# Two pairs per output product, and the output bias moved from TensorE to POOL

## The reference

```python
x = x + tanh(g_xattn[0]) * xattn(layernorm(x), ctx_1024, ctx_1024, Wq, Wk, Wv, Wo)   # 16 heads of 64
x = x + tanh(g_ffn[0]) * ffn(layernorm(x), ...)

def ffn(x):
    h = rmsnorm(x, gamma1)
    q = (h @ Wq + bq).reshape(b, t, 16, 8)
    kv = ((h @ Wdown + bdown) @ Wup + bup).reshape(b, t, 16, 16)
    k, v = split(kv, 2, axis=-1)
    att = softmax(einsum('bthd,btgd->bthg', q, k) / sqrt(8))
    x = x + (einsum('bthg,btgd->bthd', att, v).reshape(b, t, 128) @ Wo + bo)
    h2 = rmsnorm(x, gamma2)
    gate = softmax(h2 @ Wg + bg)                        # 8 experts
    return x + einsum('btd,edf,bte->btf', h2, We, gate)
```

## Time and profile before

| | us |
|---|---|
| three runs | 260.14, 260.2, 263.66 |
| median | 260.2 |
| the profiled execution | 261.93 |
| its span | 259.9 |

### The profile page before, as it was taken

How to read it: one execution, slowest core, us unless ns; L and a number is a source line. 1 busy time by engine, 2 the same in 40 slices (tenths; PEclk the granted TensorE clock), 3 DMA queues, 4 the chain that set the end, 5 groups by cost and what they waited for, 6 DMA issues and landing times.

```text
span 259.9 us, 7887 instructions
## 1 busy us (share of the span) xinstructions
PE 245.6 (94%) x3244; PEld 178.7 (69%) x3244; DVE 192.4 (74%) x333; ACT 171.6 (66%) x501; POOL 149.9 (58%) x157
## 2 busy tenths in 40 slices
PE   7989989998899999999999999988999897979995
PEld 4765877785867677676859595858676462858774
DVE  0237644189998989898998842799989999786964
ACT  2437634756687787978787778566877676472454
POOL 4104041264646686969696835778466995867320
PEclk9999999999999999999999999999999998899999
DMA  6990000000000000000000000000000000000000
GB/s 208 359 320 21 3 4 3 3 1 3 3 3 0 3 10 3 15 0 15 1 3 13 3 11 3 13 3 10 3 0 5 11 14 3 11 0 3 10 13 20
DMA packets 6017, 7.30 MB, mean 28 GB/s; under 512 B 477, under 2 KB 4830, under 8 KB 5982
## 3 DMA queue, kind: packets, MB, share of 16 engines
q1 hardware_dynamic: 5550, 6.16, 7.5%
q10 hardware_dynamic: 432, 0.64, 0.7%
HBM read 5.88 MB, written 0.92 MB: 26 GB/s over the span
## 4 chain that ended last, share of the span: by engine, by line
PE 70%; DVE 18%; ACT 5%; issue 4%; POOL 1%; DVEq 0%; POOLq 0%
PE ps_a L875 40%; PE ps_c L875 9%; PE ps_b L875 8%; PE ps_e L875 7%; PE ps_b L927 4%; DVE ps_e L665 3%; DVE prod L683 3%; DVE ps_e L694 2%; ACT probs L446 2%; DVE nmax L626 2%; PE ps_b L872 1%; DVE psums L631 1%; DVE fqkv L649 1%; POOL prod L326 1%; PE ps_c L971 1%
## 5 line engine op out<-in xcount | busy, mean ns | idle before, releaser
L326 POOL TENSOR_TENSOR prod<-fqkv 128x1280 f32<-128x1280 f32 (+1 forms) x14 | 38.7, 2761 | 10.3 <-DVE fqkv L649 10.3
L316 POOL TENSOR_TENSOR probs<-probs,prinv 120x672 f32<-120x672 f32 x16 | 24.3, 1518 | 31.1 <-DVE prinv L635 31.1
L334 POOL TENSOR_TENSOR prod<-e_sb,fqkv 128x768 f32<-128x768 f32 (+1 forms) x14 | 24.5, 1753 | 21.3 <-ACT e_sb L474 21.3
L875 PEld LDWEIGHTS ps_a<-aT,wo_sb 128*128 128x128 f32 x256 | 30.8, 196 | 4.4 <-ACT v_sb L435 2.6
L875 PE MATMUL ps_a<-aT,wo_sb 128*128 128x112 f32 x256 | 32.1, 279 | 0.4 <-ACT aT L440 0.3
L875 PE MATMUL ps_a<-wv_sb,cT 128*64 128x512 f32 x128 | 32.3, 620 | 0.0
L665 DVE TENSOR_REDUCE ps_e<-prod 128x256 f32<-128x2048 f32 x13 | 29.7, 2287 | 0.0
L694 DVE TENSOR_REDUCE ps_e<-prod 128x128 f32<-128x2048 f32 x13 | 29.7, 2285 | 0.0
L875 PE MATMUL ps_a<-cT,wk_sb 128*128 128x224 f32 x128 | 28.6, 375 | 0.0
L429 ACT COPY kT<-ps_a 128x448 f32<-128x448 f32 x32 | 17.1, 533 | 16.2 <-PE ps_a L875 16.2
L875 PE MATMUL ps_a<-xT,wqc 128*128 128x224 f32 x128 | 27.1, 361 | 0.6 <-ACT qT L429 0.6
(11 more groups left out here) (144 smaller groups left out, 487.9 us busy)
## 6 DMA issues: line engine op xcount, KB each, us to landing
xp_sb<-in_xp SPq DMA_DIRECT2D x1, 896.0 KB, 7.9
out<-out_sb SPq DMA_DIRECT2D x14, 64.0 KB, 1.5
xT<-in_x_t SPq DMA_DIRECT2D x1, 784.0 KB, 9.5
cT<-in_ctx_t SPq DMA_DIRECT2D x1, 784.0 KB, 11.1
wv_sb<-in_wv SPq DMA_DIRECT2D x1, 512.0 KB, 8.1
wo_sb<-in_wo SPq DMA_DIRECT2D x1, 512.0 KB, 12.7
fwe_sb<-in_fwe SPq DMA_DIRECT2D x1, 512.0 KB, 8.8
fw_sb<-in_fw SPq DMA_DIRECT2D x1, 266.0 KB, 13.1
```

The lines of the kernel that those rows point to most:

```text
L316: nc.gpsimd.tensor_tensor(pr[0:TG, NC:C, :, 0:S], pr[0:TG, NC:C, :, 0:S], prinv[p % 2][0:TG, NC:C, :].unsqueeze(3).to_broadcast([TG, C - N ...
L326: nc.gpsimd.tensor_tensor(o, k, q, ALU.mult).then_inc(s["prod1_pool"], 1)
L334: nc.gpsimd.tensor_tensor(o, e, v, ALU.mult).then_inc(s["prod2_pool"], 1)
L875: return nc.tensor.matmul(o, lhsT, rhs, start=start, stop=stop, skip_group_check=True)
```

## The change

Three things are changed. The output products of pairs 1-2, 5-6, 7-8 and 9-10 are made two pairs at a time, 224 columns wide; those of pairs 3, 4 and 11 to 16 stay single (`Y_UNITS`, which counts from 0). So the two buffers of aT become one with two halves. A tile can start only when the unit that completes it is there: the tiles now start in slots 2, 3, 4, 6, 7, 8, 9 and 10 to 16, and slot 5 has no new tile instead of slot 9; slots 5, 7 and 9 have no output product. The bias matmul goes: ACT scales xc by rstd2 (`scaled_x`), POOL adds bo to it (`biased`), and `new_x2` only adds. And the order within a slot is new on every engine.

```diff
-def first_step(f):
-    return (128 * (f + 1) + T - 1) // T
-TILE_AT = {first_step(f): f for f in range(NT)}
+Y_UNITS = [(0, 1), (2,), (3,), (4, 5), (6, 7), (8, 9)] + [(p,) for p in range(10, NP)]
+Y_AT = {unit[-1] + 1: n for n, unit in enumerate(Y_UNITS)}
+def units_for(f):
+    return next(n + 1 for n, unit in enumerate(Y_UNITS) if (unit[-1] + 1) * T >= (f + 1) * 128)
+def tile_steps():
+    steps, last = {}, 0
+    for f in range(NT):
+        last = max(last + 1, Y_UNITS[units_for(f) - 1][-1] + 1)
+        steps[last] = f
+    return steps
+TILE_AT = tile_steps()
...
-        aT = two("aT", [128, C, T])
+        aT = sb("aT", [128, C, 2 * T])
...
+            def biased(f):                                   # POOL
+                pool.wait_ge(s["u_ready"], f + 1)
+                if f == 0:
+                    pool.wait_ge(s["wo_scaled"], 2)
+                nc.gpsimd.tensor_tensor(xc[f % XB][:, :], xc[f % XB][:, :], fw_sb[:, COL_BO:COL_BO + D], ALU.add).then_inc(s["ub_ready"], 1)
...
+            def scaled_x(f):                                 # ACT
+                act.wait_ge(s["centred"], f + 1)
+                act.wait_ge(s["rstd2_ready"], f + 1)
+                nc.scalar.activation(xc[f % XB][:, :], xc[f % XB][:, :], ACT.Copy, scale=rstd2[f % XB][:, 0:1]).then_inc(s["u_ready"], 1)
...
             def new_x2(f):                                   # VectorE
                 dve.wait_ge(s["o_made"], f + 1)
-                nc.vector.scalar_tensor_tensor(out=x2[f % 2][:, 0:D], in0=xc[f % XB][:, :], scalar=rstd2[f % XB][:, 0:1], in1=ps_c[:, 1, 0:D],
-                                               op0=ALU.mult, op1=ALU.add).then_inc(s["x2_ready"], 1)
+                dve.wait_ge(s["ub_ready"], f + 1)
+                nc.vector.tensor_tensor(x2[f % 2][:, 0:D], ps_c[:, 1, 0:D], xc[f % XB][:, :], ALU.add).then_inc(s["x2_ready"], 1)
...
-            new_x1(0)                                        # VectorE, ahead of the slots
...
-            def new_y(p):                                    # TensorE
+            def new_y(n):
...
+                c0, w = Y_UNITS[n][0] % 2 * T, len(Y_UNITS[n]) * T
                 for ch in range(C):
-                    ins = mm(ps_a[:, 0, 0:T], wo_sb[:, ch, :], aT[p % 2][:, ch, :], start=(ch == 0), stop=(ch == C - 1))
+                    ins = mm(ps_a[:, 0, 0:w], wo_sb[:, ch, :], aT[:, ch, c0:c0 + w], start=(ch == 0), stop=(ch == C - 1))
...
-                mm(ps_c[:, 1, 0:D], ident[:, :], fw_sb[:, COL_BO:COL_BO + D], stop=False)
...
-            new_y(0)                                         # TensorE, between attend(0) and attend(1)
```

More of the change, by code:

```diff
@@ L408, in _ @@
             gating(third)
+            biased(prior)
             weighted(last)
+            biased(last)
             second_scale(prior)
@@ L545, in _ @@
                     squares(fc)
+                if t < NP:
+                    exps(t)
+                if fc is not None:
                     x2_copy(fc)
@@ L550, in _ @@
                     head_exps(fb)
+                if fc is not None:
+                    gate_exps(fc)
+                if fb is not None:
+                    scaled_x(fb)
                 if t < NP:
@@ L564, in _ @@
                     kv_copy(fa)
+                if fc is not None:
+                    experts(fc, 1)
             for t in range(TAIL, END):
@@ L586, in _ @@
             x1_copy(last)
+            squares(third)
             kv_copy(last)
+            head_exps(prior)
             x2_copy(third)
-            squares(third)
-            head_exps(prior)
-            late_out(PE_OUT[0])
+            scaled_x(prior)
             gate_exps(third)
@@ L798, in _ @@
                     new_x2(fc)
+                if fb is not None:
+                    logits(fb)
+                if t in Y_AT:
+                    new_x1(Y_AT[t])
                 if t < NP:
                     prob_sums(t)
-                if t <= NP:
-                    new_x1(t - 1)
-                if t < NP:
                     norm(t)
                 if fb is not None:
-                    logits(fb)
                     shifted_logits(fb)
@@ L847, in _ @@
             weighted(prior)
+            gate_logits(third)
             logits(last)
-            gate_logits(third)
+            gate_sum(third)
             shifted_logits(last)
             head_scales(prior)
-            gate_sum(third)
             normed_heads(prior)
             weighted(last)
+            head_scales(last)
             new_x2(prior)
-            head_scales(last)
             head_sums(last)
@@ L1099, in _ @@
                 if t < NP:
+                    values(t, 1)
+                if fc is not None:
+                    new_o(fc)
+                if t < NP:
                     shift(t)
-                if fc is not None:
-                    bias_o(fc)
-                    new_o(fc)
-                if t <= NP:
-                    new_y(t - 1)
+                if t in Y_AT:
+                    new_y(Y_AT[t])
                 if fc is not None:
@@ L1118, in _ @@
                     first(fa)
+                if t < NP:
+                    turn_probs(t)
                 if fc is not None:
```

119 lines of the change are left out of this document (57 added, 62 removed).

## The result

The changed kernel took 266.06 us, the median of 263.31, 265.8, 266.31 and 266.41, against 260.17 us for the kernel before, measured beside it: a ratio of 1.019, with an interval of 1.015 to 1.023. The forecast was 257.2, and its range ended at 261.8. One thing has to be known to read these numbers. The execution of 263.31 has a mean granted clock of 1.0 and a span of 261.5 us; the three others have 0.993 or 0.994 and spans of 264.0 to 264.6. On another chip (first experiment) all five executions were at 1.0, and the median was 263.06. So the change costs about 3 us by its own work, and about 3 more in executions in which the clock falls.

A forecast was written before the change was run, and what follows sets the result against it. TensorE bounds the middle, VectorE the end. Start's gain is lost by slot 5 (0.2 later), slots 5 to 13 take 123.9 against 124.4; lead 1.0, clock 0.95, waits 0.6, biases 0.45 sum to 3.0: 257.2 us, range 253.5 to 261.8.

The forecast's parts named there:

- attend(1): Sign in the start: with the first output product gone, attend(1) starts at 34.5 us instead of 37.17.
- the wide product: Sign in slot 2: one output product of 16 records, 224 columns wide, takes about 3.2 us.
- the chain behind the logit sums: Sign at the end: the last tile's chain after logit_sums stays the 26 us that it is now.
- the 202 that was to prove the forecast wrong: Sign: slot 14 starts about 200.4; before 199 or after 202, the forecast is wrong.
- Start, -2.6 and +1.4: Start and slot 2: removing the first product gives -2.6 us; the wider product costs +1.4, plus a 0.5 wait.
- Slots 3 and 4: Early slots: the second projection waits for new_x1 behind the logits, about 1.1 and 0.8 us; slot 5 starts 0.2 later.
- Pairing, -1.5: Output products made two pairs at a time save 0.37 us for each of four pairs, 1.5 in all.
- F: Time from a slot's start to the end of VectorE's scaled_qkv: 1.6 us in slot 9, forecast to fall to about 1.05.
- Bias, -3.2: Every tile: removing TensorE's 28 bias records saves 0.23 us a tile, 3.2 in all; ACT and POOL have room.
- POOL's queue as the loop: Rival, chance 0.22, middle slots: norm behind outputs in POOL's queue sets the slot, 12.4 + F; slower than before, 263.5 us.
- End, -3.0: From slot 14 on VectorE sets the pace: 1.0 lead, 0.95 clock, 0.6 waits, 0.45 biases, 3.0 us in sum.
- 0.95 of clock: End: the clock's drop near 219 us, costing 1.9 us, was taken as coming every second time: -0.95.

The follow-up runs named there:

- first experiment: The changed kernel run again unaltered on another chip: 263.06 us, ratio 1.010 to the kernel before.
- r_after_free: The changed kernel with eight tiny matmuls placed where TensorE waits for ACT in the start: 263.99 us against 260.61 for the kernel before, 1.012.
- c_single: The changed kernel with every output product made for one pair again, the first back between attend(0) and attend(1): 263.06 us, 1.008 to the kernel before.
- d_bias: The kernel before with only the bias moved from TensorE to ACT and POOL: 262.24 us, 1.007.
- b_values: The changed kernel with TensorE doing both values together and the shift ahead of new_o: 266.34 us, 1.022 to the kernel before.
- i_first_pad: e_first with eight tiny matmuls added to TensorE's warm-up: 261.99 us against 260.42 for the kernel before, 1.006.
- j_before_pad: The kernel before with eight tiny matmuls added to TensorE's warm-up: 266.4 us, 1.023.
- e_first: The kernel before with only the first output product removed from the start and merged with the second in slot 2: 264.31 us against 259.91, 1.016.
- h_oldbias: The changed kernel with TensorE's bias matmul back, right ahead of new_o: 267.2 us, 1.025 to the kernel before.
- f_pairs: The kernel before with output products merged as in the change, orders and bias old: 265.64 us, 1.021.
- k_best: e_first with the change's orders from slot 14 on, bias kept on TensorE: 264.16 us, 1.014 to the kernel before.
- p_free: e_first with eight tiny matmuls placed where TensorE waits for ACT in the start: 259.48 us against 259.95 for the kernel before, 0.996.

## Why the prediction was wrong, step by step

The span was forecast at 256.9 us and took 261.5 at a full clock, 4.6 more. Of this, 1.0 was there when slot 5 began and 3.5 came in slots 5 to 13; the end took what it was given. Of the signs that the prediction named, attend(1) (34.14), the wide product (3.03) and the chain behind the logit sums (26.2 us) came as forecast; slot 14 started at 205.10, beyond the 202 that was to prove the forecast wrong.

**Start, -2.6 and +1.4.** Both right. Counted from pair 0's scores, the product's removal brings slot 2 forward by 22.75 - 20.19 = 2.56 us; the other 0.47 of the table's difference is chance. The wide product takes 3.03 to the next start (3.17 forecast). The half microsecond of waiting for turned probabilities is there (0.69).

**Slots 3 and 4.** The wait for x1 behind the logits was forecast at 1.1 and 0.8, and is 1.29 (in r_after_free and c_single; in the changed kernel's slot 3 the pause stands in its place) and 0.73. But the sum left them out in part: its own terms make -0.7 + 1.1 + 0.8 = +1.2 for slot 5's start, and it wrote 0.2 without saying what would take up the other 1.0. Nothing did: slot 5 started 1.17 later in the profiled execution, and 1.64 later counted from pair 0's scores, 0.5 of it the pause, which no row of before shows.

**Pairing, -1.5.** The product itself was priced a little too high: a pair's slot is 1.14 us longer than a single one (1.4 forecast), and a merge saves 2 x 1.77 - 3.03 = 0.51 of product time. By the rule of the Trainium skill on loading the weights (TensorE: Matmul & The Clock Gate, LDWEIGHTS) it would have been 1.7; the row of the projections was the better guide, and the trace gives these loads a median of 192 ns each, not the rule's 107. It is the slots without a product that don't shrink as much as forecast. Slots 5, 7 and 9 took 13.86, 11.47 and 13.66; forecast were 13.2, 10.9 and 13.1, each 0.6 short. POOL's norm was named as what TensorE waits for, and it is (1.05, 0.87 and 0.51). What the step lacked is that the norm has a wait of its own. The forecast let it start when POOL's queue gets to it and end 8.4 after F; in slot 9 it then waits 0.20 us for VectorE's reciprocal of the sums (the row of 141.76), in slot 5 0.39, in slot 7 0.38, since those sums now stand behind the logits. In slot 5 that wait hangs on a pause of 0.21 us in the scores: in r_after_free, which has neither, slot 5 takes 13.39, and slot 9, which has such a pause there, 14.18.

**Bias, -3.2.** This is the step that failed in kind, with what it was to give in every slot of the middle (0.23 x 9). It was priced by its own duration, half of a piece of the chain, and nobody was named who would be late next. d_bias shows who: ACT's copy of the turned heads. In the change the second half of the values covers that copy, and cutting the values in two costs time: values and turned heads take 180.22 - 177.95 = 2.27 us, against 121.77 - 119.74 = 2.03 before. That is +0.24, and b_values gets it back by putting them together. From there to the product it is 180.93 - 180.22 = 0.71 against 122.62 - 121.77 = 0.85: the bias's -0.14, not -0.23. The projections add 0.13 (182.81 to 186.10 against 124.50 to 127.66). So a single product's slot takes 14.15, where 13.7 was forecast and 13.91 had been. The 3.5 us between the forecast's 123.9 for slots 5 to 13 and the 127.45 measured are 3 x 0.45 of this, 1.8 of the slots without a product and 0.4 of the pairs' (15.29 against 15.1, 15.44 against 15.4, 15.29 against 15.1).

**POOL's queue as the loop** (0.22, 263.5 us) came nearest in time but not in kind. Its condition was that F stays at 2.1. F in slot 9 was 134.06 + 0.61 - 133.71 = 0.96, near the forecast's 0.85, and in slots 11 to 13 TensorE has no wait for POOL at all. That its time was near is luck.

**End, -3.0.** From slot 14's start to the end it took 56.4 us instead of 59.1, 2.7 less, where the forecast's terms behind slot 14's start make 2.6: right in the sum, and misread in what it is taken from. In executions without the fall of the clock the old orders take 26.58 us from slot 14 to y(15) (i_first_pad: 228.84 - 202.26; j_before_pad too) and not 27.82, so of the 2.7 only 1.4 is the change's. The forecast subtracted 0.95 of clock from an execution of 261.93 and then gave 257.2 against a median of 260.2, most of whose executions had no fall to give back.

**The sum** for executions at a full clock: -2.6 to slot 2's start, +1.8 in slot 2, +1.7 in slot 3, +0.6 in slot 4, +3.1 in slots 5 to 13, -1.4 at the end: +3.3 (from unrounded values). Measured, on the chip where all executions of the changed kernel were at a full clock: spans of 261.1 to 261.9, median 261.3, against a median of 258.1 for the kernel before's at a full clock: +3.2.

**The clock: open.** The rest of the 5.9 us goes with the lower clock of three executions, and no trace of them exists. That the fall comes with the pause is likely: with the pause three of the changed kernel's nine executions had it, though all three on one chip, and without it none of eight. Where it falls, and by what it costs 3 us, is not known. In e_first and b_values it falls right behind the pause (0.59 and 0.64 of full clock over 50 to 54 us; the values take 3.05 instead of 1.94), and b_values' span is then 0.8 to 1.0 above its executions at a full clock. In h_oldbias, the nearest relative, it falls in slot 15, and the span is 2.6 above its execution at a full clock, as in the changed kernel (2.5 to 3.1). In the changed kernel, f_pairs and k_best the traces have the pause and no fall at all.

**Left open too:** what decides whether a block of instructions comes in time. The kernels run here fit the rule that it is the place of the blocks against the short matmuls: the six without the first product (changed, b_values, e_first, f_pairs, k_best, h_oldbias) pause in slot 3 behind the same record, and those with it or with the tiny matmuls don't pause there, though all of those but before and p_free have a pause somewhere else, mostly of 0.2 to 0.8 us. How far ahead a block is asked for isn't shown. Nor is it shown how the 0.24 of a full slot would divide under a third set of orders.

## What to carry over

An operation on the busiest engine is worth its duration only if the next thing that engine needs is ready earlier too; before you price a removal, write down the producer of that next thing, and when it is done. Where four engines' orders have been fitted to each other, an order is priced with its partners: the orders of two engines taken across cost 14 us here, and that of one 21, though the whole new set costs 3. A wait that has been priced must also stand in the sum. And the sum starts from an execution with the same clock as the median's.

## What was not expected of the hardware

TensorE can stand inside a row of short matmuls without any wait in the program. The pauses were 0.2 to 2.0 us long, all in the scores or the attended values (64 records in 1.00 to 1.16 us), and they went or came with eight matmuls more in the first 22 us. In the changed kernel a packet of instructions of 0.02 MB moves between 48.0 and 48.5 us, at slot 3's start; in the kernel before the one ahead of slot 3 moves at 41.5 to 42.0, and none between 42 and 50. In all six kernels with the pause in slot 3 a packet moves within 0.4 us of that slot's first matmul, and TensorE goes on 2.2 to 2.9 us after the packet. The page gives this queue 26 packets and 0.43 MB for the whole program, of whose 7887 instructions TensorE has 6488, and in the changed kernel 25 packets for 6304; so it is probably TensorE's own, with some 250 instructions to a packet (an estimate from these counts). Behind a pause of 1.97 us the granted clock averaged 0.59 over the next 4 us in e_first, and stayed at 1.00 in h_oldbias. Fp32 matmuls of 8 columns took 0.2 us each in the warm-up and 0.12 (1.18 us for 10) in the first queries' wait.
